# Earlier requests for the half tiles' second-layer weights, and for their table, in a mixture-of-experts kernel

## What is computed

```
h = tokenizer(x)                                   # 128 x 124 tokens of 256
h = h + attention(layernorm(h))                    # one head, within a sequence
h = h + moe(layernorm(h))

# moe: per token
logits = softmax(relu(f @ router_w1 + b1) @ router_w2 + b2)      # 6 experts
top_w, top_i = top_k(logits, 2);  gate = softmax(top_w)
h1 = relu(f @ expert_w1[e] + expert_b1[e])                       # 256 -> 256
h2 = relu(h1 @ expert_w2[e] + expert_b2[e])
y  = h2 @ expert_w3[e] + expert_b3[e]
moe = sum over the two chosen e of gate * y
```

## Time and profile before

| | |
|---|---|
| three runs, median | 1242.8 us |
| lowest, highest | 1240.68, 1245.06 us |
| profiled execution | 1239.83 us |
| its span, first to last instruction | 1238.0 us |
| mean granted TensorE clock | 0.988 of full speed |
| busy share PE, PEld, DVE, ACT, POOL | 96%, 85%, 79%, 66%, 71% |
| transfers of half_sb | 33, 512 KB each |

### The profile page before, as it was taken

One profiled execution on the slowest core, in us unless ns is written; L12 is line 12 of the kernel. 1 busy time (PEld: TensorE's weight loads), 2 busy tenths in 40 slices (PEclk: granted clock), 3 DMA queues, 4 the chain that ended last, 5 costly groups with the idle time before them and its releaser, 6 DMA issues.

```text
span 1238.0 us, 27898 instructions
## 1 busy us (share of the span) xinstructions
PE 1182.6 (96%) x7784; PEld 1050.3 (85%) x7784; DVE 977.5 (79%) x3290; ACT 819.2 (66%) x1967; POOL 880.0 (71%) x674
## 2 busy tenths in 40 slices
PE   6999999999999999999889999999999999999994
PEld 5888988898889888988678888989988888899983
DVE  5678888888888888887688786788877787788773
ACT  4788888888888888886445554645655655555542
POOL 2227888888888788887788675766775786677566
PEclk9999999999999999999899999999999999999997
DMA  3324655454445445654589979877888788887865
GB/s 121 123 91 125 161 149 151 122 134 127 126 122 136 126 127 140 175 161 125 131 191 279 238 135 273 174 141 148 175 214 208 149 172 197 214 164 165 223 122 60
DMA packets 146470, 195.49 MB, mean 158 GB/s; under 512 B 38920, under 2 KB 104204, under 8 KB 146316
## 3 DMA queue, kind: packets, MB, share of 16 engines
q1 hardware_dynamic: 71036, 125.04, 32.9%
q0 software_dynamic: 74016, 67.88, 32.7%
q10 hardware_dynamic: 1264, 0.79, 0.2%
HBM read 162.79 MB, written 99.09 MB: 212 GB/s over the span
## 4 chain that ended last, share of the span: by engine, by line
PE 62%; SPq 10%; issue 8%; ACT 7%; DVE 5%; POOL 4%; DMA 3%; POOLq 0%; ACTq 0%; DVEq 0%
PE bank L961 18%; PE bank L752 16%; PE bank L989 9%; SPq L496 6%; PE bank L906 4%; PE bank L807 3%; PE bank L892 3%; POOL expert_rows L666 3%; PE bank L950 3%; DMA half_sb<-split_weights 2%; PE bank L798 2%; PE bank L852 2%; PE bank L914 1%; SPq L503 1%; ACT rec L1056 1%
## 5 line engine op out<-in xcount | busy, mean ns | idle before, releaser
L735 POOL DMA_INDIRECT out<-yo,tail x236 | 378.1, 1602 | 133.7 <-issue 73.3
L666 POOL DMA_INDIRECT expert_rows<-rec,row_i x256 | 355.0, 1387 | 78.0 <-issue 67.0
L1172 ACT ACTIVATE h2v<-bank,small 128x512 f32<-128x512 f32 x118 | 81.3, 690 | 226.4 <-PE bank L961 205.6
L989 PE MATMUL bank<-w_sb,h_hi 128*128 128x256 f32 x944 | 186.4, 290 | 3.3 <-issue 3.3
L961 PE MATMUL bank<-h_hi,w_sb 128*128 128x512 f32 x472 | 157.0, 393 | 3.9 <-issue 3.6
L961 PE MATMUL bank<-x_hi,w_sb 128*128 128x512 f32 x472 | 157.0, 394 | 3.5 <-DVE x_lo L1613 2.9
L989 PEld LDWEIGHTS bank<-w_sb,h_hi 128*128 128x128 f32 x944 | 153.0, 194 | 4.0 <-issue 3.9
L989 PE MATMUL bank<-w_sb,h_lo 128*128 128x256 f32 x472 | 134.6, 285 | 0.0
L752 PE MATMUL bank<-tok_proj,xT_hi 128*124 128x256 f32 x512 | 101.1, 290 | 9.0 <-DVE tok_proj L1198 9.0
L961 PEld LDWEIGHTS bank<-h_hi,w_sb 128*128 128x128 f32 x472 | 88.8, 188 | 23.4 <-issue 5.5
L961 PEld LDWEIGHTS bank<-x_hi,w_sb 128*128 128x128 f32 x472 | 89.4, 189 | 22.5 <-issue 3.1
(11 more groups left out here) (243 smaller groups left out, 3104.7 us busy)
## 6 DMA issues: line engine op xcount, KB each, us to landing
w_sb<-split_weights SPq DMA_DIRECT2D x165, 512.0 KB
xg<-expert_rows SPq DMA_DIRECT2D x59, 530.0 KB
half_sb<-split_weights SPq DMA_DIRECT2D x33, 512.0 KB
out<-h SPq DMA_DIRECT2D x32, 496.0 KB
split_weights<-half_w SPq DMA_DIRECT2D x36, 256.0 KB
x_in<-in_x SPq DMA_DIRECT2D x32, 250.0 KB
small<-in_esmall SPq DMA_DIRECT2D x59, 134.0 KB
raw_w<-in_eweights SPq DMA_DIRECT2D x36, 128.0 KB
```

Of the source, the lines that this page charges most:

```text
L666: pool.indirect_dma_start(rows_dram, bass.IndirectOffsetOnAxis(ap=row_i[0:TOK, slot, j, k:k + 1], axis=0), rec[0:TOK, slot, j, :], None).t ...
L735: pool.indirect_dma_start(out, bass.IndirectOffsetOnAxis(ap=kept_tail(t)[:, j, E8:].bitcast(I32), axis=0), sums_out(t)[:, j, :], None, com ...
L989: mm = pe.matmul(banks[6 + b][:, i * D:(i + 1) * D], act[:, c, j * P:(j + 1) * P], w[:, 2, c, wh, :], start=(c == 0 and p == 0), stop=(c = ...
L1172: act.activation(h2v[:, m, 0:cols], banks[bank + m][:, 0:cols], ACT.Relu, bias=small_in(t)[:, DC + m:DC + m + 1]).then_inc(S["h2_v"], 1)
```

## The change

The half tile's layers are asked for one in each full tile: layer 1 at `since == 1`, layer 0 with the rows at `since == 2` as before, and layer 2 alone at `since == 3`. The table's three steps move from t=10, 11 and 12 to t=8, 9 and 10, since layer 1 of half tile 0 now needs the table at t=11.

```diff
             def half_loads(t):
 
-                if t == FIRST_HALF - HALF_STEP:
+                if t == FIRST_HALF - HALF_STEP - 2:
                     sp.wait_ge(S["halves"], HALVES_AT)
                     sp.dma_start(half_dram, u_coli[0:NH, :]).then_inc(S["half_tab_kept"], 16)
-                if t == FIRST_HALF - HALF_STEP + 1:
+                if t == FIRST_HALF - HALF_STEP - 1:
                     sp.wait_ge(S["half_tab_kept"], 16)
                     sp.dma_start(half_tab[:], half_dram.rearrange("(o t) k -> o (t k)", o=1)
                                  ).then_inc(S["half_tab_loaded"], 16)
-                if t == FIRST_HALF - HALF_STEP + 2:
+                if t == FIRST_HALF - HALF_STEP:
                     sp.wait_ge(S["half_tab_loaded"], 16)
                 for k in range(NH):
                     since = t - (FIRST_HALF + HALF_STEP * (k - 1))
+                    if since == 1:
+                        half_layers(k, (1,))
                     if since == 2:
                         half_rows(k)
                         half_layers(k, (0,))
                     if since == 3:
-                        half_layers(k, (1, 2))
+                        half_layers(k, (2,))
```

## The result

| | before | the change |
|---|---|---|
| first comparison, 5 runs each: median us (lowest to highest) | 1243.98 (1240.68 to 1245.58) | 1234.99 (1233.49 to 1237.66) |
| ratio, 95% interval | | 0.9941 [0.9917, 0.9964] |
| second comparison, 30 and 12 runs | 1242.34 (1236.61 to 1245.67) | 1237.19 (1233.52 to 1242.2) |
| ratio, 95% interval | | 0.9961 [0.9946, 0.9976] |
| profiled execution of the first | 1239.83, span 1238.0 | 1237.66, span 1235.9 |

The change makes the kernel faster: by 7.3 us (4.5 to 10.3) in the first comparison, and by 4.8 us (3.0 to 6.7) in the second and larger one. 4.0 us were forecast, which is inside the second interval and just outside the first. The profiled execution before took less than any of its five timed runs and that of the change was the slowest of its five, so the spans alone would show only 2.1 us.

A forecast was written before the change was run, and what follows sets the result against it. The prediction took TensorE to be the bound, with SyncE's queue late before it. Its terms, -5.74 + 1.2 + 0.6 = -3.9, say -4.0 us, from the median 1242.8 gave 1238.8 us, range 1235 to 1244.

The forecast's parts named there:

- What bounds the kernel: Expert phase: TensorE, busy for 96% of the span, is the bound; SyncE's queue is late through half tile 0.
- The waits for `half_sb`: Second layers of half tiles 0, 4, 7 and 10: all four waits for weights go, -5.74 us.
- Half tile 0's rows: Before half tile 0's first transposes: rows requested 1.2 us later, PE stands 3.2 us instead of 2.00, +1.2 us.
- Layer 2 of full tile 54: Weights request near half tile 10: leaves later, at 1169.4, and lands after its use at 1174.55, +0.6 us, upper end 1.9.
- The prediction's own alarm: New waits for half_xg or w_sb over 4 us together, or SyncE never waiting from 780 on, would refute the queue term.
- queue term: SyncE's queue: one more table read and the moved issue cost 1.2 us, 0.6 us net for each half tile.
- SyncE's waits fall by 0.6 us a half tile: SyncE's waits on the tail copies, 11.5 us before, fall by some 0.6 us for each half tile.
- rival (a): Low-clock stretch after half tile 0's wait for rows: a second adds 1.7 us, or it falls away, -1.7; chance 0.12 each.
- (b): Lateness moves to half tile 10's rows, tile 54's layer 2 or half tiles' layer 0: 1240.6 to 1242.3 us; chance 0.18.
- (c): SyncE's added time exceeds its 2.0 us wait per half tile and it never catches up: 1249 us; chance 0.05.
- (d): The new layer 1 request waits for something and blocks SyncE's queue: 1244.0 us; chance 0.05.

The follow-up runs named there:

- E3: Kernel before with the table's three steps two tiles sooner and two unused table reads added per half tile, all transfers in old places; 1250.70 us, ratio 1.0069.
- E4: The change, with a half tile's expert number read once and kept in a register; 1233.44 us, ratio 0.9955.
- E9: E4 with the full tiles' two numbers (`EXPERT`, `NEW_W`) also read once a tile and kept; 1244.44 us, ratio 1.0032.
- E6: Kernel before with layer 1 requested with layer 0 at `since == 2`, table in its old place, no read added; 1236.14 us, ratio 0.9953.
- E8: Kernel before with the half tile's expert number read once and kept, old order of requests; 1239.32 us, ratio 0.9982.
- E2: Kernel before with only the table's three steps moved two tiles sooner; 1241.27 us, ratio 1.0005.
- E5: The change again, without an edit; 1237.19 us, ratio 0.9961.
- E11: Kernel before, unchanged, third trace; 1248.27 us in one run.
- E7: E4 repeated without an edit, in another group; 1235.15 us, ratio 0.994.
- E1: Kernel before, unchanged, second trace; 1245.02 us in one run.

## Why the prediction was right, point by point

**What bounds the kernel.** Right: PE is the bound up to the end, and SyncE is late in front of it. E3, E4 and E9 show it from both sides: reads added without a transfer cost some 9 us, reads removed with no transfer moved take PE's idle time from 4.8 and 4.9 us to 0.4 and 2.5, and with more of them removed (E9) SyncE stands 9.8 us ahead of PE at half tile 0 for 1.0. Two of the prediction's readings were short of the view: beside the 5.7 us for `half_sb` the view of the earlier trace rows has 3.6 us on "issue", 3.1 of it at 647.3, where the expert phase is entered and the change does nothing; and the view of the earlier trace rows has a second line of 1.5 us. Neither changes the sum.

**The waits for `half_sb`, -5.74 us.** Right in kind and place. All four are gone in both traces of the change, and E6 and E8 show that it is the earlier request that removes them. They were larger in the other traces of before (6.2 and 10.4 us), so the term, taken from one trace, was probably too small for an average execution.

**Half tile 0's rows, +1.2 us.** The measured wait is 3.12 us for a forecast 3.2, and 3.02 the second time. Taken against the 2.00 us of the first trace that is +1.1. This agreement is luck. The mechanism had the request leave 1.2 us later and PE stand that much longer. In this pair it left 1.66 us later, but PE, too, was ready 1.66 us later, and the 1.12 us are the transfer's, which took 4.14 us to its use for 3.02. That is not the fault of the 512 KB under way: in E2, where nothing new is under way, the rows took 4.0 us as well. The queue's part of the term is borne out: SyncE's way to this request lasted 89.1 us twice, for 85.5 to 88.2 in the seven traces without the call, so 0.9 to 3.6 us more (1.5 in the pair), and E3 shows 88.5 with the reads alone. But three traces of before have waits of 2.00, 0 and 2.23 us, so no single pair could have tested a term of 1.2.

**Layer 2 of full tile 54, +0.6 us.** This term was mis-sized: 1.67 and 1.89 us measured. The place and the mechanism were right. In the first trace the lead was no worse than forecast: the request left 5.5 us before PE was ready (1167.05 to 1172.55), for 5.2 in the prediction (1169.4 to 1174.55) and 6.3 before; in E5 it was 4.6. It took 7.13 and, in E5, 6.44 us instead of the 5.73 that the prediction took over from its neighbour. Over twelve traces this transfer took 5.8 to 7.8 us, and 9.3 in E9. The term's upper end of 1.9 held.

**The prediction's own alarm.** It said that new waits for `half_xg` or `w_sb` of over 4 us together would make its queue term wrong. Counted whole they are 4.8 us, and 4.9 in E5, where the forecast itself comes to 3.8; counted by what they grew they are 2.8, for 1.8. So on the first count the alarm sounded. What exceeded the forecast was the time of the second transfer, with, in E5, a smaller lead, and not what the added call costs SyncE.

**SyncE's waits fall by 0.6 us a half tile.** The sign as I had put it, less time in the view of its waits, did not come: 13.8 us after 11.5. The view lists a part only. The gaps between its instructions fell by 5.8 us over ten half tiles, 0.6 each, which looks like the amount. It does not prove it: the same sum is 20.2, 24.1 and 27.0 us in three traces of before and 14.4 and 11.9 in the change, and SyncE follows PE, which was through this part 3.9 us sooner. The direction is shown, the size of 0.6 is not.

**The clock, rival (a).** In the pair of traces it gave nothing, as the sum had it: one low stretch before, one after. Over all traces it can be weighed better than it was. "Rest" in the table is 468.2 to 468.8 us without a low stretch, 470.0 to 471.1 with one (3.4 us), 472.1 to 472.4 with two and 474.8 with four. By the means of these groups that is 2.0, 1.9 and 1.6 us each, where 1.7 was worked out; a single trace scatters by more (1.5 to 2.7 for one). So a wait that brings one costs its own length and about 1.7. Which waits do is clear for the longer ones, within the stretch: all twelve of 2.56 us and more did. Of the eleven from 1.62 to 2.35 us one did, the 2.00 us of the earlier trace rows, from which the prediction had its doubt; and behind the stretch the wait of 2.01 us before the last third layer, the same in every trace, is followed within 1.3 us by 3.4 us at 1.2 GHz in five traces (before, E11, E4, E7, E8) and in the others not. So for a wait of 2 us these traces give no rule. The Trainium skill, "TensorE: Matmul & The Clock Gate", section "HAM oscillation", has it that waits on DMAs put the array back to the low clock. The traces agree for the longer waits and only now and then for the shorter. The waits for `half_sb` brought two such stretches in E1, two in E11 and one in E2, none in the first trace; the change loses them and has one at its longer wait for the rows. Beside E1 and E11 that is one stretch less, a gain that the sum had at nothing.

**The other rivals.** (b), the wait passes on, happened in part: 1.7 and 3.1 us stand where 7.7 stood. (c), SyncE becomes the bound, did not happen to the change, but E3 shows how near it was: two reads more for each half tile with the requests in their old order, and waits over 3 us stand at half tiles 4 and 7. (d), it doesn't do what it says, is refuted by the request at 728.77.

**The sum.** -5.74 + 1.12 + 1.67 = -2.95 us of idle time, where -3.94 was forecast; the stretch as a whole gave -3.9, and the 1.0 between them lies in "rest" (471.1 and 470.2), within what traces with one low stretch differ by. So that the stretch gives just the -3.9 of the sum is luck, too: a microsecond too much was forecast of the idle time, and a microsecond that no term held made up for it. The medians gave -4.8 in the larger comparison. The remaining 2.5 us of the first comparison's 7.3 did not come again; their cause is open. The prediction was right in what bounds the kernel, in where the waits go and in the sign of each term; its number is nearer than its terms were.

## What to carry to other kernels

An engine that only issues transfers can be the one that is late. Count its reads and register steps a tile as you count a compute engine's instructions, and measure a request's lead from where that engine really stands in its program. Moving the request saved some 5 us here, and reading a number once and keeping it, by itself, some 2 (E8). This went on until the next resource in line, the ordered adds, was full: with still fewer reads (E9) the kernel was slower, though TensorE got to its last layer 6.6 us sooner than in the change. And before a difference of a few microseconds between two traces is given to a cause, see how much the same wait differs between two traces of one kernel.

## What the runs showed of the hardware

- One 512 KB transfer, the request for layer 2 of full tile 54, took 5.8 to 7.8 us from issue to landing over twelve traces, beside a DMA share of 1.07 to 1.14 in that time; in the thirteenth, E9, it took 9.3 (share 1.09). The rows of half tile 0, half as many bytes, took 3.0 to 4.1 us, and 4.7 in E9.
- SyncE's unbroken way to one request, the same instructions each time (in E2 three of them two tiles sooner), took 85.5 to 88.2 us in seven traces.
- A stretch of 3.4 us at 1.2 instead of 2.4 GHz cost PE 1.6 to 2.0 us by the means of the groups of traces, and their number alone sorts the thirteen traces by PE's time without idle gaps.
- GpSimd's indirect adds that must wait for an earlier one to land stood 3.0 to 3.2 us at best, and up to 6.7 us; issued without such a wait they follow each other every 1.84 us.
